# A gated-linear-attention and FFN layer on one core: where two norms get their epsilon, when o is measured, which engine takes two remainders, and when x2 and u are transposed

## The reference

```python
q, k, v = x@Wq, x@Wk, x@Wv                     # 16 heads of 8 channels
gate = exp(log_sigmoid(x@Wgk1@Wgk2 + bgk2)/16)
state = state*gate + v*k ; o = sum_k state*q   # one step per token
o = (o - mean)/sqrt(var + 1e-5)*gamma + beta   # var, mean over 128 channels
x = layernorm(x + (o*silu(x@Wg)) @ Wout)       # called x2 below
h = silu(x@w1.T*s1) * (x@w2.T*s2)              # 512 wide, layer 0 below
h = gelu(h@h1.T*sh1) ; h = gelu(h@h2.T*sh2)    # layers 1 and 2
x = layernorm(x + h@w3.T*s3)
```

## Time and profile before

| what | value |
|---|---|
| median of 3 runs | 179.91 us (179.28 to 179.99) |
| the profiled execution | 179.08 us, of which the span is 177.2 us |
| TensorE busy | 159.9 us, 90% of the span |
| VectorE busy | 139.4 us, 79% |
| ScalarE busy | 117.2 us, 66% |
| GpSimd busy | 110.2 us, 62% |
| TensorE clock granted | 1.0 throughout |
| chain that ended last, by engine | PE 28%, DVE 21%, issue 9%, ACT 4%, POOL 2% |

### The profile page before, as it was taken

One profiled execution on the slowest core, in us unless ns is written; L12 is line 12 of the kernel. 1 busy time (PEld: TensorE's weight loads), 2 busy tenths in 40 slices (PEclk: granted clock), 3 DMA queues, 4 the chain that ended last, 5 costly groups with the idle time before them and its releaser, 6 DMA issues.

```text
span 177.2 us, 2661 instructions
## 1 busy us (share of the span) xinstructions
PE 159.9 (90%) x778; PEld 119.0 (67%) x778; DVE 139.4 (79%) x286; ACT 117.2 (66%) x211; POOL 110.2 (62%) x101
## 2 busy tenths in 40 slices
PE   0899999999879999999899999889999999999980
PEld 0766657868657666877667677467666875886870
DVE  0689989968898997698999967989996795864062
ACT  4454889992147635388687458567978588996621
POOL 8705998969709689971577999708686340705032
PEclk9999999999999999999999999999999999999999
DMA  3999920244100000000000000000002000031102
GB/s 114 303 366 412 401 85 0 59 122 118 59 4 0 0 2 0 4 2 0 0 0 0 0 0 0 0 0 0 0 4 61 0 0 0 2 86 51 59 4 63
DMA packets 7455, 10.55 MB, mean 60 GB/s; under 512 B 753, under 2 KB 5394, under 8 KB 6930
## 3 DMA queue, kind: packets, MB, share of 16 engines
q1 hardware_dynamic: 6866, 7.50, 13.7%
q0 software_dynamic: 576, 2.88, 4.2%
HBM read 8.55 MB, written 1.84 MB: 59 GB/s over the span
## 4 chain that ended last, share of the span: by engine, by line
PE 28%; DVE 21%; issue 9%; ACT 4%; POOL 2%; DVEq 1%; POOLq 0%
DVE state L1144 6%; PE ffn L661 5%; PE ffn L652 4%; DVE f_lo L1243 3%; DVE y L1156 2%; PE ffn L718 2%; PE att L699 2%; PE att L687 2%; PE ffn L630 2%; PE ffn L711 2%; PE ffn L635 2%; ACT f_hi L938 2%; PE att L585 1%; DVE x L1180 1%; POOL o_rstd L364 1%
## 5 line engine op out<-in xcount | busy, mean ns | idle before, releaser
L1144 DVE TENSOR_TENSOR_SCAN state<-gate,att 128x512 f32<-128x512 f32 x32 | 38.4, 1209 | 2.2 <-PE att L574 2.2
L400 POOL TENSOR_TENSOR f_lo<-full,f_hi 128x512 fp32r<-128x512 f32 x18 | 23.0, 1293 | 25.1 <-DVE full L1232 18.1
L938 ACT ACTIVATE f_hi<-ffn,vec_cols 128x512 fp32r<-128x512 f32 x24 | 16.5, 688 | 19.8 <-PE ffn L661 19.6
L652 PE MATMUL ffn<-f_hi,h_hi 128*128 128x512 f32 x96 | 28.1, 407 | 0.2
L661 PE MATMUL ffn<-f_lo,h_hi 128*128 128x512 f32 x96 | 26.1, 399 | 0.0
L345 POOL TENSOR_TENSOR u_tok<-kv_tok 128x1024 f32<-128x1024 f32 x12 | 25.5, 2137 | 0.1
L360 POOL TENSOR_TENSOR o_acc<-o_acc,y 128x512 f32<-128x512 f32 x16 | 20.7, 1291 | 7.6 <-DVE y L1156 7.5
L652 PEld LDWEIGHTS ffn<-f_hi,h_hi 128*128 128x128 f32 x96 | 17.6, 188 | 5.8 <-ACT f_hi L938 1.5
L574 PE MATMUL att<-ident,u_tok 128*128 128x128 f32 x128 | 19.3, 277 | 1.7 <-DVE state L1144 1.2
L661 PEld LDWEIGHTS ffn<-f_lo,h_hi 128*128 128x128 f32 x96 | 17.8, 188 | 3.7
L574 PEld LDWEIGHTS att<-ident,u_tok 128*128 128x128 f32 x128 | 15.3, 142 | 6.3 <-DVE state L1144 3.3
(11 more groups left out here) (188 smaller groups left out, 356.2 us busy)
## 6 DMA issues: line engine op xcount, KB each, us to landing
h_raw<-in_hT SPq DMA_DIRECT2D x2, 1024.0 KB, 12.3
h_hi<-in_hT POOLq DMA_DIRECT2D x2, 1024.0 KB, 12.1
x_tok<-in_x SPq DMA_DIRECT2D x4, 256.0 KB, 5.8
out<-out_tok SPq DMA_DIRECT2D x3, 256.0 KB, 2.5
w_raw<-in_w12T SPq DMA_DIRECT2D x1, 512.0 KB, 5.5
w_hi<-in_w12T POOLq DMA_DIRECT2D x1, 512.0 KB, 9.3
q_swap<-q_hi SPq DMA_DIRECT2D x3, 128.0 KB, 2.5
q_swap<-q_lo SPq DMA_DIRECT2D x3, 128.0 KB, 2.4
```

The source lines that it names most:

```text
L400: nc.gpsimd.tensor_tensor(lo[:, o], full_block(layer, o), hi[:, o].bitcast(F32), ALU.subtract).then_inc(pool_rested, 1)
L652: nc.tensor.matmul(bank[:], h_hi[:, layer - 1, c, tile(o)], src_hi[:, c], start=(c == 0), stop=False)
L938: nc.scalar.activation(hidden[layer][0][:, o], bank[:], ACT.Gelu, scale=scales[:, 1 + layer, o:o + 1]).then_inc(gelu_hi_ready, 1)
L1144: nc.vector.tensor_tensor_scan(state[:, k % 3], gate[:, b], A[2 + k % 2][:], 0.0, ALU.mult, ALU.add).then_inc(scanned, 1)
```

## The change

The epsilon of two norms (o and x2) goes from VectorE to GpSimd. VectorE measures o before it applies the gate, and `transpose_o` comes before `center_o`. Block (1,1) goes from GpSimd to VectorE, and (2,3) the other way. `transpose_x2` goes ahead of `ffn_out_hi`, and the next row's first `transpose_u` and `replicate_q` ahead of `ffn_out_rest`. On GpSimd the last norm's variance and rstd go to the end of `attention_end`.

```diff
-        ON_POOL = [(0, 0), (0, 1), (0, 2), (1, 0), (1, 1)]
-        ON_DVE = [(0, 3), (1, 2), (1, 3), (2, 1), (2, 0), (2, 2), (2, 3)]
+        ON_POOL = [(0, 0), (0, 1), (0, 2), (1, 0), (2, 3)]
+        ON_DVE = [(0, 3), (1, 1), (1, 2), (1, 3), (2, 0), (2, 1), (2, 2)]
...
+            def with_eps(b, mv, mv_ready, var, var_ready):
+                pool.wait_ge(mv_ready, TILES * (b + 1))
+                nc.gpsimd.tensor_tensor(var[:], mv[:, :, 1], eps[:], ALU.add).then_inc(var_ready, 1)
...
             def o_rstd_of(b):
+                with_eps(b, o_mv, o_mv_ready, o_var, o_var_ready)
...
             def r_rstd_of(b):
+                with_eps(b, r_mv, r_mv_ready, r_var, r_var_ready)
...
             def attention_end(a, tiles, last_tiles):
                 o_rstd_of(a)
+                outer_products(a + 1, tiles)
+                r_rstd_of(a)
+                outer_products(a + 1, last_tiles)
+                if a >= 1:
+                    rest(a - 1, 2, 3)
                 if a >= 2:
                     e_var_of(a - 2)
                     e_rstd_of(a - 2)
-                outer_products(a + 1, tiles)
-                r_rstd_of(a)
-                outer_products(a + 1, last_tiles)
             def ffn_middle(b, follows):
                 sum_over_k(b + 1, range(3, DH - 2))
                 rest(b, 1, 0)
-                rest(b, 1, 1)
...
             def first_layer(b, f, with_lo, follows):
-                if follows:
-                    transpose_u(b + 1, 0)
-                    transpose_u(b + 1, 1)
-                    replicate_q(b + 1, 0)
...
                 ffn_hidden(f, 2, 0, with_lo)
+                transpose_o(a)
                 center_o(a)
-                transpose_o(a)
                 ffn_hidden(f, 2, 1, with_lo)
...
+                transpose_x2(a)
                 ffn_out_hi(f, with_lo)
-                transpose_x2(a)
+                if follows:
+                    transpose_u(a + 1, 0)
+                    transpose_u(a + 1, 1)
+                    replicate_q(a + 1, 0)
                 ffn_out_rest(f)
                 first_layer(a, f, with_lo, follows)
...
             def ffn_silu(b, o):
+                if o == 0 and b >= 1:
+                    act.wait_ge(*rested(b - 1, 2, 3))
...
+                if (layer, o) == (2, 3):
+                    act.wait_ge(*rested(b, 1, 0))
...
-                dve.wait_ge(mv_ready, TILES * (b + 1))
-                nc.vector.tensor_tensor(var[:], mv[:, :, 1], eps[:], ALU.add).then_inc(var_ready, 1)
...
                 last_sums(a)
+                rest(f, 1, 1)
+                o_token_stats(a)
+                o_aggregate(a)
+                apply_gate(a)
                 rest(f, 1, 2)
-                apply_gate(a)
-                o_token_stats(a)
                 rest(f, 1, 3)
-                o_mean_and_variance(a)
             def make_x2(a, f):
                 add_x(a)
-                rest(f, 2, 1)
                 rest(f, 2, 0)
                 x2_normalise(a)
+                rest(f, 2, 1)
                 rest(f, 2, 2)
-                rest(f, 2, 3)
                 rest_of_x2(a)
```

More of the change, by code:

```diff
@@ L806, in rows @@
                 transpose_x2(0)
+                transpose_u(1, 0)
+                transpose_u(1, 1)
+                replicate_q(1, 0)
                 first_layer(0, None, with_lo, True)
@@ L1168, in token_stats, with aggregate @@
                     nc.vector.bn_stats(stats[:, j], bank[:, tile(j)]).then_inc(stats_ready, 1)
-            def mean_and_variance(b, stats, stats_ready, mv, mv_ready, var, var_ready):
+            def aggregate(b, stats, stats_ready, mv, mv_ready):
                 dve.wait_ge(stats_ready, TILES * (b + 1))
@@ L1185, in o_token_stats, with o_aggregate @@
                 token_stats(b, A[2], o_stats, o_stats_ready)
-            def o_mean_and_variance(b):
-                mean_and_variance(b, o_stats, o_stats_ready, o_mv, o_mv_ready, o_var, o_var_ready)
+            def o_aggregate(b):
+                aggregate(b, o_stats, o_stats_ready, o_mv, o_mv_ready)
             def add_beta_part(b):
@@ L1214, in add_x @@
                 token_stats(b, A[0], r_stats, r_stats_ready)
-                mean_and_variance(b, r_stats, r_stats_ready, r_mv, r_mv_ready, r_var, r_var_ready)
+                aggregate(b, r_stats, r_stats_ready, r_mv, r_mv_ready)
             def x2_normalise(b):
@@ L1258, in e_mean_and_variance @@
                 dve.wait_ge(e_shift_ready, b)
-                mean_and_variance(0, e_stats, e_stats_ready, e_mv, e_mv_ready, e_var, e_var_ready)
+                aggregate(0, e_stats, e_stats_ready, e_mv, e_mv_ready)
+                dve.wait_ge(e_mv_ready, TILES)
+                nc.vector.tensor_tensor(e_var[:], e_mv[:, :, 1], eps[:], ALU.add).then_inc(e_var_ready, 1)
                 nc.vector.tensor_scalar(e_minus[:], e_mv[:, :, 0], -1.0, 1.0, ALU.mult,
@@ L1356, in _ @@
             o_token_stats(0)
-            o_mean_and_variance(0)
+            o_aggregate(0)
             apply_gate(0)
```

## The result

The changed kernel takes 182.86 us, the median of 4 runs (182.29 to 184.3), beside 179.84 for the kernel before; the ratio is 1.0207, with a 95% interval of 1.017 to 1.0245. It is slower by about 3 to 3.7 us. Run again beside the experiments (e5_changed_again) it had 183.36, ratio 1.0225 (1.0189 to 1.0262). The prediction was 183.4.

What follows compares the result with a forecast made beforehand. VectorE bounds scans to o; from o to the next scan, x2's chain and TensorE's layer 2 run side by side. 0.15 + 1.41 + 0.38 + 1.98 = 3.9 us slower: 183.0 or 183.8, middle 183.4, range 181.2 to 185.5.

Steps and rivals of the forecast that it cites:

- The new wait: In layer 2, TensorE's second block waits for VectorE's `rest(1,2)`, now behind the gate, and starts 2.28 us later.
- faster: Rival, 6%: TensorE held under 0.7 us, so the sooner o_rstd counts; 2.0 us gained, 177.1 to 177.9.
- o's chain: After o_acc: gate 1.03 us later, o_rstd 1.06 sooner, `add_x` 0.67 later, the sooner o_rstd worth nothing.
- x2_hi behind the last Gelu: End of layer 2: x2_hi waits for a Gelu 2.28 us later, at 81.87 instead of 79.97; first scan 1.04 later.
- the losses of steps 1 and 2: Terms of the sum for the first two steps: 1.41 us lost in step 1, 0.38 in step 2.
- The stall of step 2: At x2's norm: VectorE's epsilon of 0.98 us and TensorE standing 0.69 disappear, cutting step 2's loss by 1.03.
- Step 3: Last step, ending in TensorE's work: `ffn_out_rest` waits for GpSimd's (2,3); layer 0's second block starts 1.98 us later.
- TensorE's lateness: Rival, 10%: carried whole from layer 2, layer 0 2.23 us later in step 1; 5.6 slower, 184.6 to 185.5.
- The epsilon: Norms of o and x2: 0.19 us on GpSimd against VectorE's 0.17; each move lengthens its chain 0.1 to 0.15.
- The clock: Rival, 2%: TensorE idle 2.0 us, its clock falls to 1.2 GHz for layer 2's rest; 6.4 a step, above 200.
- four terms of the sum: Whole kernel: prologue 0.15, step 1 1.41, step 2 0.38, step 3 1.98; together 3.9 us slower.

Runs made afterwards that it cites:

- e5_changed_again: The changed kernel as it is, nothing altered, run again beside later experiments: 183.36 us, ratio 1.0225 to the kernel before.
- e1: Changed kernel with only `rest(1,2)` put back ahead of o's statistics on VectorE: 178.41 us, ratio 0.9963 to the kernel before.
- e8: e1 with block (1,1) back on GpSimd and (2,3) back on VectorE: 179.75 us, ratio 1.0015 to the kernel before.
- e10: e1 with the epsilons of both norms (o and x2) back on VectorE: 179.43 us, ratio 1.0004 to the kernel before.
- e2: Kernel before with only the new order around o, its epsilon still on VectorE, ahead of the gate: 190.99 us, ratio 1.0658.
- e4: Changed kernel with TensorE's tail in its old order, `ffn_out_hi` first, u and `replicate_q` last: 187.74 us, ratio 1.0483 to the kernel before.
- e6: e1 with the gate put ahead of o's aggregation on VectorE: 177.44 us, ratio 0.9905 to the kernel before.
- e3: Changed kernel with the epsilons of both norms (o and x2) back on VectorE: 185.03 us, ratio 1.0319 to the kernel before.

## Why the prediction was right

**The new wait** was the deciding step, and it held: 2.28 forecast for TensorE's second block of layer 2, 72.67 - 70.46 = 2.21 measured, of which 0.09 is the later start of step 1. e1 shows that without it the kernel is not slower; the first rival on the other side ("faster") would have needed a hold under 0.7.

**o's chain.** The gate was forecast at 71.34 and is at 71.30, o_rstd's end at 72.97 and is at 72.93, `add_x` at 74.92, to the digit. The last digits are partly luck, since step 1 starts 0.09 later than in the forecast. That the sooner o_rstd is worth nothing is seen in `add_x`'s new releaser. Without the hold it counts: in e8 o_rstd is 1.5 later and the steps 0.43 to 0.93 longer.

**x2_hi behind the last Gelu** held: 81.87 forecast, 81.72 measured. x2_hi starts 0.58 after the last Gelu does (81.14, 81.72), not at its end, 0.69; this is 0.1 of the 0.15 by which the first scan (82.94) came sooner than the forecast's 83.09, and yT is at 84.63 for 84.7. The second product of layer 0 was forecast 1.41 later; it is 1.40 later (86.93 against 85.53), and the third, with the third scan right behind it, 1.34 (88.31 against 86.97). Less the 0.09 by which step 1 starts later, that is 1.25. So the mis-sized terms are the losses of steps 1 and 2: 1.25 for 1.41, and 0.25 for 0.38.

**The stall of step 2** is gone, as forecast, and both steps now take the same, 34.16 and 34.19 for 34.3. **Step 3**: its second block of layer 0 starts at 152.91, 3.49 later than the earlier trace rows, and the span is 3.42 longer, so that next to nothing is gained or lost after it. The trace shows no wait for yT ahead of that block, as the forecast had it; yT, up to 152.86, is just in time. Of this 1.9 is step 3's own, for 1.98. There the move of (2,3) to GpSimd showed as the forecast said: TensorE waits 0.49 for it.
```profile
151.64 0.50 PE L683 MATMUL ffn<-f_lo,w_hi 128*128 128x512 f32 x1 [0.49 <-POOL f_lo L406]
```

**TensorE's lateness** was not carried whole: layer 0 started 2.17 later in step 1 (84.43 for 82.26), the next o_acc 1.34. From the first scan to o TensorE was busy for 18.27 of 19.45 and is now for 19.32 of 19.91, so its idle time there halved, from 1.2 to 0.6. How much more lateness the scans could take up, no run shows.

**The epsilon** on GpSimd takes 0.20 to 0.21, VectorE's 0.16 to 0.17 with nothing beside it. The ratio of 1.96 that the GPSIMD Engine Reference of the Trainium skill (Elementwise) has for an addition is not seen at this size. Its own length matters less than its place: by the ratios e10 is 0.7 us slower than e1, since an epsilon on VectorE delays the gate, by 0.28 in any step and by 0.57 where it stands behind an outer product.

**The clock**, given 2%, stayed granted at 1.00 in the steps of both profiled executions of the changed kernel. Two of its first four runs had more time and a lower mean clock (spans 181.4 at 0.992 and 182.5 at 0.984); a low stretch is likely in the second, but neither was profiled. e2 to e4 show that the danger was real and suggest that 2% was too little. They also show that the prediction priced it far too high: it let all the rest of layer 2 run at 1.2 GHz, 6.4 a step and a total above 200, where a stretch at half the clock cost 1.3 to 1.6.

**The number.** The span was forecast 3.9 longer and is 3.4 longer; by the profiled execution that is 183.0 forecast and 182.41 measured. All four terms of the sum were somewhat too large. The forecast of 183.4 is as far from the median, 182.86.

## What to carry to other kernels

Before moving an instruction behind others on its engine, ask who waits for it on another engine, and what is queued there behind the waiting one: here a remainder of 0.68 us that frees a bank was the dearest to delay. If a reordering makes a chain shorter and the kernel slower, look for the one wait that it adds; here one line, put into a time in which VectorE waited anyway, turned 2% slower into 0.4% faster (e1), and a second one, the gate ahead of the aggregation, made it 1% (e6). Look at where a small operation with two SBUF inputs on VectorE falls beside long ones of GpSimd: the same addition took 0.16 us alone and up to 1.76 beside an outer product (e2). Before a profiled span is used to price a part, see where it lies among the spans of all runs of its kernel.

## What the runs showed that I had not expected

The granted clock fell to half after holds of less than 2 us, with TensorE busy before and after: in e4 after 1.91 and 1.95, but not after the 1.88 of its step 1, and in none of the changed kernel's profiled steps with the same holds (1.88 to 1.95). The length of the hold alone does not decide either: in e3 the clock fell after 2.21 us in step 1, and not after 2.50 in step 2 and 2.26 in step 3. Windows of e3 behind the holds of steps 1 and 2:
```profile
74.00:77.40 3.40, 3.40 (x14) 2.92 (x13) 1.77 (x8) 0.16 (x1) 0.64 (x1) 0.51 0.00 0
109.11:112.50 3.39, 3.39 (x19) 2.95 (x20) 1.67 (x5) 0.28 (x1) 1.90 (x1) 1.00 0.00 0
```
The page TensorE: Matmul & The Clock Gate of the Trainium skill (The HAM clock gate) ties the fall to an idle array and calls the observation free-running, which would fit a matter of phase; no run here shows what decides. Where it fell it cost 1.3 (e3) to 1.6 us (e4) a time, about as much again as the 1.5 a step of the hold.
